# Local attention in a six-stage decoder: the scores of two key blocks merged in PSUM into one 128x128 tile per head, the diagonal carried apart, the upper triangle selected on GpSimd

## The reference, cut to what matters

```python
q, k, v = heads(x @ Wq.T), heads(x @ Wk.T), heads(x @ Wv.T)
# query block i (128 rows) sees key block i-1 (c < 128) and its own (c >= 128)
dist = bs + r - c                       # r: row in the block, bs = window = 128
valid = (dist >= 0) & (dist <= window) & (key_global >= 0)
scores = where(valid, q @ kw.T / sqrt(8), lowest)
out = softmax(scores) @ vw @ Wo.T
```

## Time and profile before

| | us |
|---|---|
| median of 3 runs | 473.54 (471.21 to 473.64) |
| span of the profiled execution | 473.8 |
| busy: PE / DVE / ACT / POOL | 388.1 / 303.7 / 215.5 / 118.4 |
| item 0 of the loop begins | 146.8 |
| last norm instruction of stage 4 ends | 239.2 |

### The profile page before, as it was taken

The page is one execution under the profiler, slowest core; times in us unless marked ns, Lnnn a source line. Parts: engine busy times, 40 slices in busy tenths (PEclk is TensorE's granted clock), DMA queues, the critical chain, the costliest instruction groups (busy, mean ns, idle before and its releaser), DMA issues.

```text
span 473.8 us, 6810 instructions
## 1 busy us (share of the span) xinstructions
PE 388.1 (82%) x2387; PEld 225.7 (48%) x2387; DVE 303.7 (64%) x611; ACT 215.5 (45%) x551; POOL 118.4 (25%) x215
## 2 busy tenths in 40 slices
PE   5996969389987999999754867768676998999993
PEld 2645457244434566576532223333344544665572
DVE  4984498959624697878646979989871362132235
ACT  2664221272235765855214789899881311111100
POOL 8248646828460000000080111212110000000002
PEclk9989895779988899999985589998975698999997
DMA  8992110670000000000000999999982004011211
GB/s 244 318 361 25 1 2 1 223 310 1 0 1 0 1 3 0 2 1 1 2 0 13 265 169 172 155 163 173 131 162 51 0 0 143 24 44 49 63 44 44
DMA packets 75521, 39.84 MB, mean 84 GB/s; under 512 B 64160, under 2 KB 71264, under 8 KB 75040
## 3 DMA queue, kind: packets, MB, share of 16 engines
q1 hardware_dynamic: 73184, 39.35, 34.1%
q0 software_dynamic: 2304, 0.07, 1.4%
HBM read 21.58 MB, written 2.88 MB: 52 GB/s over the span
## 4 chain that ended last, share of the span: by engine, by line
PE 53%; DVE 15%; DMA 12%; ACT 10%; issue 5%; POOL 4%; SPq 0%; POOLq 0%; ACTq 0%; DVEq 0%
PE ps L762 27%; ACT area_b L692 7%; PE ps L1162 6%; DMA area_b<-area_b 6%; PE ps L945 5%; PE ps L956 5%; PE ps L975 3%; DMA area_a<-area_b 3%; POOL deltas L490 2%; PE ps L939 2%; DMA area_b<-deltas 1%; DVE area_a L1275 1%; DMA deltas<-entry_w,small 1%; ACT area_a L673 1%; DVE stats L1282 1%
## 5 line engine op out<-in xcount | busy, mean ns | idle before, releaser
L1535 DVE CUSTOM_DVE_ANT_0 area_a<-ps,zero,small 128x1024 f32<-128x1024 f32 x64 | 79.4, 1278 | 9.7 <-ACT area_b L692 5.0
L692 ACT ACTIVATE area_b<-area_a,small 128x1024 int16<-128x1024 f32 x64 | 73.0, 1142 | 11.3 <-DMA area_b<-area_b 5.9
L673 ACT ACTIVATE area_a<-ps,small 128x256 f32<-128x256 f32 (+1 forms) x128 | 51.9, 432 | 31.0 <-DVE small L1426 28.7
L459 POOL TENSOR_SCALAR var_eps<-meanvar 128x1 f32<-128x1 f32 x24 | 6.6, 273 | 225.3 <-DVE meanvar L1283 225.2
L762 PE MATMUL ps<-xT_odd,early 128*128 128x512 f32 x128 | 59.5, 613 | 0.0
L1054 PE MATMUL ps<-area_b 128*128 128x512 bf16 x128 | 45.0, 446 | 13.5 <-DVE small L1535 12.4
L1593 DVE TENSOR_TENSOR area_b<-ps,area_b 128x512 f32<-128x512 f32 x16 | 11.1, 691 | 55.7 <-ACT area_b L737 55.7
L1426 DVE TENSOR_REDUCE small<-ps 128x4 f32<-128x1024 f32 (+1 forms) x24 | 29.3, 1222 | 18.3 <-PE ps L945 18.1
L737 ACT ACTIVATE area_b<-ps 128x512 f32<-128x512 f32 x16 | 9.5, 596 | 67.2 <-PE ps L762 67.2
L762 PE MATMUL ps<-area_b,xT_even 128*128 128x512 f32 x64 | 31.1, 631 | 9.0 <-ACT area_b L650 9.0
L762 PEld LDWEIGHTS ps<-xT_odd,early 128*128 128x128 f32 x128 | 25.0, 197 | 27.1 <-issue 26.6
(11 more groups left out here) (265 smaller groups left out, 667.4 us busy)
## 6 DMA issues: line engine op xcount, KB each, us to landing
early<-in_w_up_dram SPq DMA_DIRECT2D x1, 4096.0 KB, 16.1
area_b<-gates_out SPq DMA_DIRECT2D x16, 256.0 KB, 3.0
deltas<-area_b SPq DMA_DIRECT2D x1, 2112.0 KB, 17.8
area_b<-deltas SPq DMA_DIRECT2D x2, 1024.0 KB, 5.9
area_a<-in_w_down_dram SPq DMA_DIRECT2D x1, 2048.0 KB, 8.5
early<-in_ctxT_dram SPq DMA_DIRECT2D x1, 1024.0 KB, 13.1
early<-in_ctx_dram SPq DMA_DIRECT2D x1, 1024.0 KB, 14.0
early<-in_w_qkv_dram SPq DMA_DIRECT2D x2, 384.0 KB, 5.1
```

The lines of the kernel that those rows point to most:

```text
L673: a = act.activation(p1[:, n % 2, x * nk * P:(x + 1) * nk * P], scores1(n)[:, x * nk * P:(x + 1) * nk * P], ACT.Exp, bias=nmx1[:, n % 2, x ...
L692: act.activation(px[:, u % PX, :], sx[:, u % 3, :], ACT.Exp, bias=nbx[:, u:u + 1], accum_out=zx[:, i, h:h + 1]).then_inc(sem("px_ready"), 1)
L1535: dve.tensor_tensor_reduce(sx[:, u % 3, :], bank(2 * (u % 2), 2), zero[:].broadcast_to([P, B * M]), qsc[:, i, h:h + 1], LOWEST, ALU.add, A ...
```

## The change

Row r needs the keys c >= r of the block before and c <= r of its own: one 128x128 square for each head, except that on the diagonal both count. In tiles 1 and 3 the change packs the two blocks into one square. Column c holds the score with its own block for c <= r and with the block before for c > r; the score with the block before at c = r, the diagonal, is handled apart. Tiles 0 and 2 keep their mask and their work.

- **PE**: in tiles 1 and 3 no mask matmul; two score matmuls of 512 columns in place of four of 256; 4 transposes for an item in place of 8; `apply` takes the packed square times the values of the own block, and the upper triangle of the square times the difference of values (block before minus own), 8 + 8 matmuls where 16 were. After the last item of tiles 1 and 3 two more matmuls add the diagonal's part. Before the loop's third item 4 small matmuls make the diagonal's scores (`diagonal`).
- **DVE**: in place of one maximum over 1024 columns: a predicated copy of 4x128 within PSUM (the block before over the own block, where `upper` is set), a maximum over 4x128, and a 128x4 minimum with the negated diagonal score, one behind the other; one copy of 128x512 into `pT1` in place of two. Before the loop, two products q times k of 128x256 (`diag_prod`); a small copy `take_diagonal`; one addition of the diagonal's part to the row sums in `invert_z`.
- **ACT**: 4 Exps of 128 columns in place of 4 of 256. Its copies of k wait for `diag_prod`. After items 11 and 23 it has one Exp of 128x32 on `diag_p`, which waits for POOL.
- **POOL**: two differences of values of 128x1024, a select of 128x512 for each of the 16 items (`upper_half`), and at the end of tiles 1 and 3 a subtraction of 128x32 and four products of 8x8 a row. Its constants at the start change a little: `window` is half as large, two of its selects go, `upper` comes.

The rest of the diff renames semaphores and joins some of them (`in_stage3`, `mix_steps`, `shared_steps`), with no other order.

```diff
-        pT1 = carve("b", 20 * N, [4, 8 * P])
+        pT1 = carve("b", 20 * N, [8, 4 * P])
+        pTU1 = carve("b", 8 * N, [4, 4 * P])
+        vdiff1 = [xT[0][:].rearrange("p c n -> p (c n)").rearrange("p (u w) -> p u w", w=HU * DH1),
+                  carve("a", 0, [H1 // HU * HU, HU * DH1])]
...
-            link(select(window[:, 0, :].rearrange("p (j k) -> p j k", k=P), [[0, 4], [-1, P]], 0, 1, ALU.is_ge, MASKED))
-            both = window[:, 1, :].rearrange("p (j b k) -> p j b k", j=2, b=2)
-            link(select(both[:, :, 1, :], [[0, 2], [-1, P]], 0, 1, ALU.is_ge, MASKED))
-            link(select(both[:, :, 0, :], [[0, 2], [1, P]], 0, -1, ALU.is_ge, MASKED))
+            link(select(window[:].rearrange("p (j k) -> p j k", k=P), [[0, 4], [-1, P]], 0, 1, ALU.is_ge, MASKED))
+            link(select(upper[:], [[1, P]], -1, -1, ALU.is_ge, 0.0))
...
+            def upper_half(n):
+                u = merged_before(n)
+                evacuated(pool, first_half(n + 1))
+                if u >= 4:
+                    pool.wait_ge(sem("o1_ps"), merged1[u - 4] // 2 + 1)
+                pool.affine_select(out=pTU1[:, u % 4, :].rearrange("p (h q) -> p h q", q=P),
+                                   in_=pT1[:, first_half(n) % 8, :].rearrange("p (h q) -> p h q", q=P), compare_op=ALU.is_ge, fill=0.0,
+                                   base=-1, pattern=[[0, 4], [-1, P]], channel_multiplier=1).then_inc(sem("pTU1_ready"), 1)
+            def diagonal(i):
+                s = i // 2
+                pool.wait_ge(sem("max1_ready"), first1[i + 1])
+                pool.tensor_tensor(out=diag_p[:, s, :], in0=nmax1[:, s, :], in1=diag_neg[:, s, :],
+                                   op=ALU.subtract).then_inc(sem("diag_steps"), 1)
+            def diagonal_values(i):
+                s = i // 2
+                pool.wait_ge(sem("diag_steps"), 3 * s + 2)
+                if s:
+                    pool.wait_ge(sem("o1_ps"), first1[i - 1] // 2)
+                prev = v1[:, (i - 1) * H1:i * H1, :].rearrange("p (t j) w -> p t j w", j=HU)
+                p = diag_p[:, s, :].rearrange("p (t j) -> p t j", j=HU)
+                pv = diag_pv[:].rearrange("p (t j d) -> p t j d", j=HU, d=DH1)
+                for j in range(HU):
+                    a = pool.tensor_tensor(out=pv[:, :, j, :], in0=prev[:, :, j, j * DH1:(j + 1) * DH1],
+                                           in1=p[:, :, j:j + 1].broadcast_to([P, H1 // HU, DH1]), op=ALU.mult)
+                a.then_inc(sem("diag_steps"), 1)
+            def local_attention():
+                for s in range(B):
+                    value_differences(s)
+                for n in merged1:
+                    last = n + 1 == first1[items1[n][0] + 1]
+                    if last:
+                        diagonal(items1[n][0])
+                        diagonal_values(items1[n][0])
+                    upper_half(n)
+                    for i in range(TT - 1):
+                        if n == first1[i + 1] + 4:
+                            inverse_deviation(4, i)
...
-                    act.wait_ge(sem("qk1_ps"), 2 * c + 2)
+                    act.wait_ge(sem("diag_prod_ready"), c + 1)
...
-                    heads = [(g, j) for g in (2 * gp, 2 * gp + 1) for j in range(hh * HU // nk, (hh + 1) * HU // nk)]
-                    for x, (g, j) in enumerate(heads):
+                        act.wait_ge(sem("pT1_ps"), first_half(n - 1))
+                    for x, (g, j) in enumerate(heads1(n)):
                         h = HU * (c * UC + g) + j
-                        a = act.activation(p1[:, n % 2, x * nk * P:(x + 1) * nk * P], scores1(n)[:, x * nk * P:(x + 1) * nk * P],
-                                           ACT.Exp, bias=nmx1[:, n % 2, x:x + 1], accum_out=z1[:, i, h:h + 1])
-                        if x % (len(heads) // 2) == len(heads) // 2 - 1:
+                        if merged(n):
+                            src, shift = scores1(n)[:, (2 * x + 1) * P:(2 * x + 2) * P], nmax1[:, i // 2, h:h + 1]
+                        else:
+                            src, shift = scores1(n)[:, x * P:(x + 1) * P], nmx1[:, n % 2, x:x + 1]
+                        a = act.activation(p1[:, n % 2, x * P:(x + 1) * P], src, ACT.Exp, bias=shift, accum_out=z1[:, i, h:h + 1])
+                        if x % 4 == 3:
                             a.then_inc(sem("p1_ready"), 1)
+                    if merged(n) and n + 1 == first1[i + 1]:
+                        act.wait_ge(sem("diag_steps"), 3 * (i // 2) + 1)
+                        act.activation(diag_p[:, i // 2, :], diag_p[:, i // 2, :], ACT.Exp).then_inc(sem("diag_steps"), 1)
...
                 def scores(n):
                     i, c, hh, gp = items1[n]
-                    nk = 1 + i % 2
                     if n >= 2:
 
-                        pe.wait_ge(sem("p1_ready"), 2 * (n - 1))
-                    heads = slice(hh * HU // nk, (hh + 1) * HU // nk)
+                        pe.wait_ge(sem("p1_ready"), first_half(n - 1))
+                    if not merged(n):
+                        for x in range(2):
+                            pe.matmul(bank(2 * (n % 2) + x), ident_b[:], window[:], start=True, stop=False)
                     for x in range(2):
-                        pe.matmul(bank(2 * (n % 2) + x), ident_b[:], window[:, nk - 1, :], start=True, stop=False)
-                    for b in range(nk):
-                        kt = i - nk + 1 + b
-                        for x in range(2):
-                            rows = slice(32 * (2 * gp + x), 32 * (2 * gp + x + 1))
-                            dst = bank(2 * (n % 2) + x).rearrange("p (j b k) -> p j b k", b=nk, k=P)[:, :, b, :]
-                            mm = pe.matmul(dst, qT1[rows, c, i * P:(i + 1) * P], kT1[rows, c, heads, kt * P:(kt + 1) * P],
-                                           start=False, stop=b == nk - 1)
+                        rows = slice(32 * (2 * gp + x), 32 * (2 * gp + x + 1))
+                        if merged(n):
+                            keys = kT1[rows, c, 2 * hh:2 * hh + 2, (i - 1) * P:(i + 1) * P]
+                        else:
+                            keys = kT1[rows, c, :, i * P:(i + 1) * P]
+                        mm = pe.matmul(bank(2 * (n % 2) + x).rearrange("p (j k) -> p j k", j=keys.shape[1]),
+                                       qT1[rows, c, i * P:(i + 1) * P], keys, start=merged(n), stop=True)
                     mm.then_inc(sem("s1_ps"), 1)
...
+                def diagonal():
+                    pe.wait_ge(sem("diag_prod_ready"), DC)
+                    pe.wait_ge(sem("const_ready"), 1)
+                    pe.wait_ge(sem("ivtok_ready"), DC)
+                    for s in range(B):
+                        for c in range(DC):
+                            mm = pe.matmul(bank(7)[:, s * H1 + c * 16:s * H1 + (c + 1) * 16], diag_prod[:, c, s, :],
+                                           head_of[:].rearrange("p g j -> p (g j)"), start=True, stop=True)
+                    mm.then_inc(sem("diag_ps"), 1)
...
+                    if not merged(2 * m):
+                        for j in range(HU):
+                            for g in range(UC):
+                                t = first_half(2 * m + g // 2) + g % 2
+                                mm = pe.matmul(dst[g], v1[:, (i * (H1 // HU) + c * UC + g) * HU + j, :], pT1[:, t % 8, j * P:(j + 1) * P],
+                                               start=c == 0 and j == 0, stop=j == HU - 1, skip_group_check=True)
+                    else:
+                        for j in range(2):
+                            for g in range(UC):
+                                t = first_half(2 * m + g // 2)
+                                at = (2 * (g % 2) + j) * P
+                                mm = pe.matmul(dst[g], v1[:, (i * (H1 // HU) + c * UC + g) * HU + 2 * hh + j, :], pT1[:, t % 8, at:at + P],
+                                               start=c == 0 and hh == 0 and j == 0, stop=False, skip_group_check=True)
+                        pe.wait_ge(sem("vdiff1_ready"), i // 2 + 1)
+                        pe.wait_ge(sem("pTU1_ready"), merged_before(2 * m + 2))
+                        for j in range(2):
+                            for g in range(UC):
+                                u = merged_before(2 * m + g // 2)
+                                at = (2 * (g % 2) + j) * P
+                                mm = pe.matmul(dst[g], vdiff1[i // 2][:, (c * UC + g) * HU + 2 * hh + j, :], pTU1[:, u % 4, at:at + P],
+                                               start=False, stop=False, skip_group_check=True)
+                        if 2 * m + 2 == first1[i + 1]:
+                            pe.wait_ge(sem("diag_steps"), 3 * (i // 2) + 3)
+                            for k in range(DC):
+                                mm = pe.matmul(bank(6)[:, k * P:(k + 1) * P], diag_pv[:, k * P:(k + 1) * P], ident[:],
+                                               start=False, stop=True, skip_group_check=True)
```

(27 more changed lines are left out.)

112 lines of the change are left out of this document (69 added, 43 removed).

## The result

| | before | changed |
|---|---|---|
| first comparison, 4 executions each | 473.59 (471.21 to 473.77) | 477.56 (476.54 to 480.88), ratio 1.0099 (1.0056 to 1.0141) |
| second, 35 and 12 | 472.96 (468.22 to 477.41) | 472.49 (465.88 to 485.01), ratio 0.9925 (0.9876 to 0.9974) |
| third, 11 and 6 | 473.24 (470.52 to 476.90) | 474.40 (472.15 to 476.86), ratio 1.0016 (0.9969 to 1.0063) |

Times are medians in us, with the lowest and highest; a ratio, with its 95% interval, is that of the fast executions alone, while a mean takes all of them. The first comparison says 0.99% slower; over all executions of the study the mean is 473.8 before (106 of them) and 474.6 changed (22), a difference of +0.8 with an interval of 1.9 to either side (the difference of means with 1.96 times its standard error; one stray execution of 1223 us is left out).

What follows compares the result with a forecast made beforehand. The prediction took PE to bound tiles 1 and 3 before the change and a DVE-POOL-PE round trip after; -9.4 - 0.5 + 2.2 + 0.9 + 0.6 + 2.4 = -3.8 from median 473.54 gave 469.7 us, range 466.5 to 476.

Steps and rivals of the forecast that it cites:

- Tiles 1 and 3, -9.4: Merged tiles of the loop: from 26.2 us each to 20.8 in tile 1 and 22.2 in tile 3, together -9.4.
- the round trip, the new bound: Merged tiles: a pair of items waits for scores, DVE's maximum and copy, POOL's select and half of `apply`, 4.79 us.
- PE is the bound no more: Merged tiles: PE's own work falls from 26.2 to about 17.9 us a tile, so something else sets the pace.
- Masks -0.5: Tile 0's stretch: the masks of items 4 and 5 go, one of them on PE's path, -0.5 us.
- small ones: Four tiny and four full-width matmuls, one DVE copy and two additions cost +0.6 us together.
- The step at item 12, +2.2: Between items 11 and 12 ACT's diagonal Exp waits for copy, select and POOL's subtraction, holding up PE too: +2.2 us.
- the clock, +2.4: Tile 2: about 3 us of PE idle at item 12 drops its clock to half, costing +2.4 us.
- the clock holds at item 12: Rival: PE's idle time at item 12 does not lower the clock, 2.4 us come back, 467.3 us; 20%.
- The end, +0.9: After item 23 the diagonal's subtraction, Exp, products, select and half `apply` take 4.5 us where 3.6 stood: +0.9.
- if stages outside the loop move: Sign that the forecast is wrong: stages outside the loop change; the sum gave no size for it.
- The dear copy: Rival: merged items' predicated copy takes 1.22 us, not 0.69, so DVE bounds the merged tiles, 476.2 us; 12%.
- PE at half clock through the merged tiles: Rival: gaps in every pair keep PE at half clock in tiles 1 and 3, some 493 us; 3%.

Runs made afterwards that it cites:

- e7: Changed kernel with the second half of `apply` in merged tiles reading the whole square, so PE waits for no select (output differs); -0.5 us against before, ratio 0.9970.
- e1: The changed kernel run and profiled again with nothing altered; mean 473.4 us.
- e2: Changed kernel with POOL's subtraction for the diagonal placed two selects earlier; mean -3.1 us against before, ratio 0.9950.
- e10: Kernel before plus 88 unread 4-column matmuls ahead of stage 5's transposes of q, moving the instruction fetch into the transfers; mean +1.3 us against before, ratio 1.0034.
- e15: Kernel before plus four small unread matmuls where the change has the diagonal's, behind the transposes of item 1; mean +2.1 us against before, ratio 1.0014.
- e3: Changed kernel with the diagonal's four small matmuls moved into PE's idle time behind the scores of items 0 and 1; mean +1.5 us against before, ratio 1.0009.
- e13: Changed kernel with early subtraction, diagonal matmuls in idle time and 34 added matmuls moving the fetch ahead of stage 5's transfers; median 469.19 us, ratio 0.9861.
- e5: The kernel before run and profiled again with no edit; six executions from 470.2 to 476.2 us.
- e4: Changed kernel with both the early subtraction and the diagonal's small matmuls in idle time; mean -1.0 us against before, ratio 0.9963.
- e8: Changed kernel with the early subtraction and ACT making the copies of the even merged items; mean -2.9 us against before, ratio 0.9939.
- e12: Changed kernel with early subtraction, 38 added matmuls moving the fetch, and ACT making the even merged items' copies; mean -5.4 us against before, ratio 0.9786.

## Why the prediction was wrong

The time: 469.7 forecast, 477.56 measured first, outside the range; some 474.6 over all executions, within the range but "the same" where I had 0.6 on faster. That the larger number of executions falls in the range is luck: two terms stood at nothing that did not stay there, and they are named below. By its steps:

- *Tiles 1 and 3, -9.4: nearly right, for the wrong reason.* Items 4 to 11 fell from 26.36 to 21.80 (-4.6, forecast -5.4); of tile 3 the first seven items give -3.9. In sum -8.5, mis-sized by 0.9. The predicated copy is as taken (0.686 for 0.69), the select a little shorter (0.656 for 0.75). But "the round trip, the new bound" failed: e7 takes the wait for it away and gains 0.00. What held in its place is what I had ruled out with "PE is the bound no more": PE is busy 15.64 of 16.04. For a pair I had PE's work about right: 4.20 in the timeline above (5.16 less 0.96 for the projection), (17.9 - 1.6) / 4 = 4.07 by my sum. For the tile I had not. PE makes scores two items ahead of its transposes, so between the scores of item 4 and those of item 12 stand the full transposes of items 2 and 3 and the mask of item 12: there go seven masks and six half transposes, 6.8 us, where I took eight of each, 8.3. PE's busy time fell by 5.3 (26.36 to 21.06 in e1); the rest, 1.5, I have not taken apart. The first place to look is the busy time of the stretch, before and behind the change.
- *Masks -0.5, and "small ones" +0.6: cancelled, as summed.* With a fall of the clock at the same moment items 0 to 3 take 13.92 before and 13.83 in e2.
- *The step at item 12, +2.2, and the clock, +2.4: right.* 2.07 us idle on ACT behind POOL's subtraction, then 0.50; 3.6 to 4.8 in three traces against 4.6, and 3.2 to 4.5 against e2, which takes only this step away. The rival "the clock holds at item 12" did not occur in them.
- *The end, +0.9: +0.2* in two traces of three (27.57 to 27.73, 27.74), +1.75 in e1, where the clock fell.
- *The step that failed: "if stages outside the loop move" stood among the signs, and at nothing in the sum.* Stage 5 takes 2.5 us more in the three traces. Fewer instructions on PE move a fetch of 16 KB of them into the stage's transfers, which costs 1.3 in its first units; e10 moves it in the kernel before and gets the same 7.3. The rest of the 2.5 goes with the clock as much as with the fetch, and stays open.
- *The second step that failed: the clock in tile 0, priced at nothing.* I counted four tiny matmuls at their duration, within the +0.6. In some executions they keep the clock at 0.50 for 17 us where it was 10.3; items 0 to 5 then take 25.1 in place of 21.9. The first profile drew this spell. Whether it is the larger scatter is not shown: e15's twelve executions scatter by 4.5 as the changed ones do, those of e3 and e13 by 3.4 and 3.5. Why the first four executions lie 4 above before, and the next eighteen do not, stays open too, as only one of the four has a trace.
- *Profile to median.* I set the summed span equal to the median. The timed figure of an execution is 1.7 above its span (475.9 and 477.63 after), so the profiled execution of before would be timed near 475.5, two above its median: it was a slow draw, with 113.7 in the last stretch where e5 has 108.1.
- The dear copy, PE at half clock through the merged tiles, and the longer select did not come. Items 6 to 11 and 16 to 22 stand at a clock of 1.00 in all but e4, e8 and e12, where it fell within items 16 to 22: in e4 from 209.3 to 216.1, 0.9 us behind a wait of PE of 0.98. The Trainium skill's "TensorE: Matmul & The Clock Gate", section "HAM oscillation — how this bites in real kernels", has kernels in which the clock falls in each wait for a transfer, waits longer than this one. Here the same wait of 0.98 stands in the changed kernel, ahead of 217.63, with the clock at 1.00 behind it: a wait as short as this does not let it fall each time.

By the means of two and three traces the stages of the change gave -3.2 where -3.8 was forecast, which is as near as such few traces can tell. What made the time come out otherwise lies in part outside, in stage 5 and in the clock; how the missing 4.6 us divide between them is not shown.

## What to carry to other kernels

Where a change takes some hundred instructions from an engine, look at where its instruction packets fall afterwards, in the transfers of stages that were not touched: with the boundary in front of the traffic the first units took 5.9 to 6.3 us, with it inside 7.2 to 7.4. Price a small matmul not only at its duration but at what the clock does around it. A small value that one engine makes for another (here a subtraction of 0.25 us) goes on the queue as soon as its input is there, not where its result is used: here that gave 3.2 us and more. And where the clock alone moves one stage by 5 us (108.1 or 113 behind stage 5), read stretches that repeat to 0.01 us in several traces, not one profile's total.

## What the runs showed of the hardware

- A predicated copy of 128x512 f32 within PSUM takes 686 ns, as a plain copy out of it does (686).
- Packets of 16 KB on the instruction queue come once for about 250 PE records. The Trainium skill's "Runtime: NRT & Kernel Launch", section "Instruction fetch mechanics", has blocks of 16 KiB or 256 instructions, with which the trace agrees, and calls the cost of crossing a boundary mostly hidden. Here it is so ahead of the traffic (fetch at 0.1 us, first units in 6.1); amid the traffic the transposes took 4.85 us for 3.64. How the fetch holds them up inside the transfer engines stays open: the slowest packets on their queue, up to 2.0 us each where before they took up to 0.7, stand 3.7 us behind it.
- Four small matmuls in the kernel before (e15) went with a spell at 1.2 GHz (0.50) of 17 us in place of 10.3. What of them does it, their few columns, their waits or their place, was not tried.
- PE idle for 2.29 us at item 12 (2.77 in e7) was followed by a fall of the clock, for 3.4 or 6.8 us, in each of the six traces that have this wait; where the wait was cut to less than 1 us the clock stayed at 1.00 through items 12 to 15.
